# A two-layer decoder on one core: the weight pairs of the context products are multiplied with each other first, the context lies in two row halves, and the planner orders the program anew

## The reference, cut to what matters

```python
# layer 0: h = ctx_512, adj_raw = x (256 x 256 for each batch)
Q, K = h @ Wq.T, h @ Wk.T                       # 64 columns
sim = Q @ K.T / (sqrt(16) * 4)                  # summed over the heads
A = sigmoid(sim) * (sim >= 76th largest of the row)
x = layernorm(x + (1 - gamma) * x + gamma * (A + A.T) / 2)
# layer 1: k_v = ctx_512, p = x
kv  = k_v @ W_k.T + b_k
out = p @ kv
sim = out @ kv.T * 256 ** -0.5
x = layernorm(x + softmax(layernorm(sim) * ln_gamma + ln_beta))
```

## Time and profile before

| | us |
|---|---|
| runs of the kernel | 700.29, 702.64, 703.87: median 702.64 |
| profiled execution, its own time | 702.17 |
| its span, first to last instruction | 700.4 |
| PE busy | 680.6 |
| DVE, ACT, POOL busy | 531.1, 494.1, 394.8 |

### The profile page before, as it was taken

The page is one execution under the profiler, slowest core; times in us unless marked ns, Lnnn a source line. Parts: engine busy times, 40 slices in busy tenths (PEclk is TensorE's granted clock), DMA queues, the critical chain, the costliest instruction groups (busy, mean ns, idle before and its releaser), DMA issues.

```text
span 700.4 us, 14717 instructions
## 1 busy us (share of the span) xinstructions
PE 680.6 (97%) x4886; PEld 574.7 (82%) x4886; DVE 531.1 (76%) x1677; ACT 494.1 (71%) x1276; POOL 394.8 (56%) x657
## 2 busy tenths in 40 slices
PE   8899999999999999999998999999989999999995
PEld 6578998888888888888886888898977787678885
DVE  2678989888697869878889776565689777866537
ACT  3789774888659784788879786646766686857631
POOL 4659732885267741698867655544791322435625
PEclk9999999999999999999999999999999999999999
DMA  8671001240341401122012002111120000101201
GB/s 293 167 229 42 17 1 40 53 122 2 109 133 32 122 1 54 46 54 61 2 49 89 1 28 63 47 46 46 46 91 3 5 2 4 48 1 46 91 1 60
DMA packets 34418, 41.06 MB, mean 59 GB/s; under 512 B 6620, under 2 KB 27238, under 8 KB 34344
## 3 DMA queue, kind: packets, MB, share of 16 engines
q1 hardware_dynamic: 33800, 39.80, 19.4%
q10 hardware_dynamic: 544, 0.33, 0.2%
HBM read 30.02 MB, written 1.05 MB: 44 GB/s over the span
## 4 chain that ended last, share of the span: by engine, by line
PE 77%; POOL 9%; DVE 8%; issue 3%; DMA 1%; SPq 1%; ACT 0%; POOLq 0%; DVEq 0%
PE bank L1184 68%; PE bank L1198 8%; POOL stat L2341 3%; POOL qT L2341 1%; PE bank L1455 1%; POOL probs L2338 1%; DMA qT<-xT_plain 1%; DVE top_tok L2238 1%; POOL probs L2341 1%; POOL w_split_lo L2341 1%; DVE g_pair_lo L1896 1%; SPq L2622 1%; DVE y L1899 1%; POOL stat L2338 1%; DVE bn L1911 1%
## 5 line engine op out<-in xcount | busy, mean ns | idle before, releaser
L2338 POOL TENSOR_SCALAR probs<-probs,soft 128x256 f32<-128x256 f32 (+1 forms) x256 | 104.5, 429 | 48.4 <-DVE soft L2031 46.7
L1686 ACT ACTIVATE probs<-probs,soft 128x256 f32<-128x256 f32 (+1 forms) x256 | 113.0, 447 | 13.5 <-DVE soft L2023 12.9
L1184 PE MATMUL bank<-xT_hi,w_split_hi 128*128 128x512 f32 x256 | 103.7, 405 | 3.5 <-POOL w_split_lo L2341 3.2
L2341 POOL TENSOR_TENSOR w_split_lo<-w_raw,w_split_hi 128x512 fp32r<-128x512 f32 (+2 forms) x57 | 72.3, 1275 | 55.1 <-ACT w_split_hi L1592 54.9
L1184 PE MATMUL bank<-xT_lo,w_split_hi 128*128 128x512 f32 x256 | 101.0, 394 | 0.0
L1184 PE MATMUL bank<-keyT,qT 128*128 128x256 f32 (+1 forms) x512 | 93.4, 330 | 0.5 <-POOL qT L2341 0.3
L2023 DVE CUSTOM_DVE_ANT_0 probs<-bank,mask 128x256 f32<-128x256 f32 (+1 forms) x256 | 78.9, 353 | 19.8 <-PE bank L1184 19.1
L1184 PEld LDWEIGHTS bank<-keyT,qT 128*128 128x128 f32 x512 | 81.8, 190 | 12.3 <-issue 2.5
L2341 POOL TENSOR_TENSOR qT<-qT,xT_plain 64x512 f32<-64x512 f32 x44 | 57.0, 1295 | 57.6 <-DMA qT<-xT_plain 55.5
L1184 PE MATMUL bank<-xT_hi,w_split_lo 128*128 128x512 f32 x192 | 75.9, 395 | 0.0
L1592 ACT ACTIVATE qT<-bank 64x512 f32<-64x512 f32 (+1 forms) x80 | 47.4, 592 | 33.1 <-PE bank L1184 30.6
(11 more groups left out here) (240 smaller groups left out, 1822.0 us busy)
## 6 DMA issues: line engine op xcount, KB each, us to landing
qT<-xT_plain SPq DMA_DIRECT2D x88, 64.0 KB, 2.0
w_raw<-in_w_nopeT SPq DMA_DIRECT2D x8, 512.0 KB, 3.6
w_raw_heads<-in_w_o SPq DMA_DIRECT2D x8, 512.0 KB, 5.1
qT<-rope_buf SPq DMA_DIRECT2D x40, 64.0 KB, 2.0
w_raw<-in_w_gateT SPq DMA_DIRECT2D x8, 256.0 KB, 2.8
w_raw<-in_w_upT SPq DMA_DIRECT2D x8, 256.0 KB, 3.3
w_raw<-in_w_downT SPq DMA_DIRECT2D x8, 256.0 KB, 3.8
w_raw<-in_L_ffn_Wup SPq DMA_DIRECT2D x7, 256.0 KB, 2.8
```

The lines of the kernel that those rows point to most:

```text
L1184: return t.matmul(out, lhsT, rhs, start=start, stop=stop, skip_group_check=shared)
L1686: ins = s.activation(p[:, at], p[:, at], ACT.Exp, bias=st[:, 0, r:r + 1], scale=-1.0, accum_out=st[:, 1, r:r + 1])
L2338: return g_.tensor_scalar(out, in0, s1, s2, op0, op1)
L2341: return g_.tensor_tensor(out, in0, in1, op)
```

## The change

Since Q K.T = h (Wq.T Wk) h.T, and kv = [c, 1] [W, b].T, the weights can be multiplied with each other first, on PE:

- a new step `mix_x`: Wq.T Wk (64 x 64, stored twice, in partitions 0 to 63 and 64 to 127), [W, b].T [W, b] (65 columns, also twice) and its last column. Three calls and two ACT copies;
- `adj_q` replaces both `adj_qk`: only one side is multiplied, by the mixed weights. `adj_sim` takes `ctxT` itself for the other;
- `ctxT` lies as 128 partitions x 512: the first two batches in the upper row half, the last two in the lower. `adj_q` and `ctx_T` issue one product of 512 columns for each half, each into its own bank;
- `ctx_tok` and its DVE add are gone: `bi_kv` multiplies the context's own rows, loaded as `ctx_rows` with a 65th column of ones (POOL memset), and gives 65 rows. The mixed weights of layer 1 make up for it in `ctx_T`, whose result `kvT` has 65 rows;
- `xattn` has four DMAs instead of six, `ctx_rows` is one more (256 KB, in pieces of 256 bytes), and `w_down0` comes by one DMA from ACT's queue instead of two;
- the warm-up waits for the memset of `ones1` alone, reads only it, and has nine products instead of eight;
- `NEAR` and the whole table `URGENT` have new values, so that every engine's order changes throughout.

```diff
-N_WARM = 8
+N_WARM = 9
-    NEAR = {"PE": 0.0, "ACT": 0.3, "DVE": 0.3, "POOL": 0.5, "SP": 0.3, "DMA": 0.1, "WAY": 0.0}
+    NEAR = {"PE": 0.05, "ACT": 0.2, "DVE": 0.3, "POOL": 0.5, "SP": 0.3, "DMA": 0.05, "WAY": 0.0}
     URGENT = {
...
-    for i in range(2):
-        stage(("adj_qk", i), "PE 1.8, ACT 1.1", ("load", "xattn"), ("load", "ctx"), By(("down_T", 1), "PE"), ...
+    stage(("mix_x",), "PE 0.6, ACT 0.5", ("load", "xattn"), holds=[bank("mix_x", left=(("mix_x",), "ACT"))])
+    stage(("adj_q",), "PE 0.95, ACT 1.1", ("mix_x",), ("load", "ctx"), ...
-    stage(("ctx_tok",), "PE 2.5, DVE 0.6", ("load", "xattn"), ("load", "ctx"), By(("down_T", 1), "PE"), ...
-    stage(("ctx_T",), "PE 1.8, ACT 1.1", ("load", "xattn"), ("load", "ctx"), By(("down_T", 1), "PE"), ...
+    stage(("ctx_T",), "PE 0.95, ACT 1.1", ("mix_x",), ("load", "ctx"), ...
-    ctxT = sb("ctxT", [CTX, T])
-    kv_tok = sb("kv_tok", [P, NT, CTX])
-    kvT = sb("kvT", [CTX, T])
+    ctxT = sb("ctxT", [P, HALF])
+    ctx_rows = sb("ctx_rows", [P, NT, CTX1])
+    kvT = sb("kvT", [CTX1, T])
...
+    def ctx_half(h):
+        return slice(h * CTX, (h + 1) * CTX)
...
-                            mm(bank_of(("low", tile))[:, :], ones1[:, :], bias1[:, 0:2 * D])
+                            mm(bank_of(("low", tile))[:, :].rearrange("p (i s) -> p i s", s=P), ones1[:, :],
+                               ones1[:, :].unsqueeze(1).to_broadcast([P, TH, P]))
...
+                mm(out[:, 0:CTX], w_q_x[:, :], w_k_x[:, :])
+                mm(out[:, CTX:CTX + CTX1], w_kv_x[:, 0:2 * CTX], w_kv_x[:, CTX:])
+                mm(out[0:CTX1, CTX + CTX1:CTX + CTX1 + 1], w_kv_x[:, CTX:], w_kv_x[:, 2 * CTX:]).then_inc(mix_x_ready.sem, 1)
...
-                    out = wait_bank(("adj_qk", i, h))[0:CTX, :]
-                    mm(out, w_qk_x[:, i, :], ctxT[:, h * HALF:(h + 1) * HALF]).then_inc(adj_qk_ready.sem, 1)
+                    rows = ctx_half(h)
+                    out = wait_bank(("adj_q", h))
+                    mm(out[rows, :], mix_x[rows, 0:CTX], ctxT[rows, :]).then_inc(mix_x_ready.sem, 1)
...
-                    mm(out, qk_x[:, 0, tile * P:(tile + 1) * P], qk_x[:, 1, cols(b)]).then_inc(sim_ready.sem, 1)
+                    mm(out, q_x[rows, first + i * P:first + (i + 1) * P], ctxT[rows, first:first + S]).then_inc(sim_ready.sem, 1)
...
-                for tile in range(NT):
-                    ins = mm(out[:, tile, :], ctxT[:, tile * P:(tile + 1) * P], w_kv_x[:, :])
-                ins.then_inc(ctx_tok_ready.sem, 1)
...
-                    out = wait_bank(("ctx_T", h))[0:CTX, :]
-                    mm(out, w_kv_x[:, :], ctxT[:, h * HALF:(h + 1) * HALF]).then_inc(ctx_T_ready.sem, 1)
+                    rows = ctx_half(h)
+                    out = wait_bank(("ctx_T", h))[0:CTX1, :]
+                    mm(out, mix_x[rows, CTX:CTX + CTX1], ctxT[rows, :]).then_inc(ctx_T_ready.sem, 1)
...
-                    ins = mm(out, kv_tok[:, TB * b + c, :], xT[:, c, cols(b)], c == 0, c == DC - 1)
+                    ins = mm(out, ctx_rows[:, TB * b + c, :], xT[:, c, cols(b)], c == 0, c == DC - 1)
...
-                    for dst, src in ((w_down0[:, :, Q0:], a["L0_attn_q_a_w"]), (w_down0[:, :, 0:Q0], a["L0_attn_kv_a_w"])):
-                        s.dma_start(dst, src.rearrange("(c p) n -> p c n", p=P)).then_inc(loaded["low"], 16)
+                    s.dma_start(w_down0[:, :, :], a["w_low"].rearrange("(c p) n -> p c n", p=P)).then_inc(loaded["low"], 16)
...
-                own(g_.memset(plain(ones1[:, :]), 1.0))
+                g_.memset(plain(ones1[:, :]), 1.0).then_inc(unit_set.sem, 1)
...
-                g_.memset(plain(bias1[:, :]), 0.0).then_inc(unit_set.sem, 1)
+                own(g_.memset(plain(bias1[:, :]), 0.0))
...
+                own(g_.memset(ctx_rows[:, :, CTX:], 1.0))
...
-            "xattn": [(w_qk_x[:, 0, :], a["L0_xattn_WqT"]), (w_qk_x[:, 1, :], a["L0_xattn_WkT"]),
-                      (gate_col[:, 0:1], a["gamma_raw"].partition_broadcast(P)),
-                      (w_kv_x[:, :], a["L1_xattn_WkT"]), (kv_bias_col[:, :], a["L1_b_col"]),
-                      (kv_bias_row[:, :], a["L1_xattn_b_k"].partition_broadcast(P))],
+            "ctx_rows": [(ctx_rows[:, :, 0:CTX], a["ctx"].rearrange("(t p) c -> p t c", p=P))],
+            "xattn": [(w_q_x[:, :], a["w_q_x"]), (w_k_x[:, :], a["L0_xattn_Wk"]), (w_kv_x[:, :], a["w_kv_x"]),
+                      (gate_col[:, 0:1], a["gamma_raw"].partition_broadcast(P))],
```

More of the change, by code:

```diff
@@ L26 @@
 CTX = 64
+CTX1 = CTX + 1
 NH, QLR, KVLR, DR, DN, DV = 32, 192, 64, 64, 128, 128
@@ L392 @@
 LOADS_AFTER = [("xT0", "xT1"), ("xT1", "xT2")] + [("xT2", name) for name in (
-    "const", "identity", "x", "ctx", "xattn", "attn1", "router")]
+    "const", "identity", "x", "ctx", "ctx_rows", "xattn", "attn1", "router")]
 def make_plan():
@@ L469, in make_plan @@
     stage(("adj_gate",), "ACT:exp 0.3, DVE 0.8", ("load", "xattn"))
-    for i in range(2):
-        stage(("adj_qk", i), "PE 1.8, ACT 1.1", ("load", "xattn"), ("load", "ctx"), By(("down_T", 1), "PE"),
-              holds=[bank("adj_qk", i, h, left=(("adj_qk", i), "ACT")) for h in range(NHALF)], items=2)
+    stage(("mix_x",), "PE 0.6, ACT 0.5", ("load", "xattn"), holds=[bank("mix_x", left=(("mix_x",), "ACT"))])
+    stage(("adj_q",), "PE 0.95, ACT 1.1", ("mix_x",), ("load", "ctx"),
+          holds=[bank("adj_q", h, left=(("adj_q",), "ACT")) for h in range(NHALF)])
     for b in range(B):
-        stage(("adj_sim", b), "PE 1.06, ACT:exp 1.55", ("adj_qk", 0), ("adj_qk", 1),
+        stage(("adj_sim", b), "PE 1.06, ACT:exp 1.55", ("adj_q",),
               *[("adj_mask", b - 1, i) for i in range(TB) if b],
@@ L482, in make_plan @@
               holds=[bank("adj_T", b, left=(("adj_T", b), "DVE"))])
-    stage(("ctx_tok",), "PE 2.5, DVE 0.6", ("load", "xattn"), ("load", "ctx"), By(("down_T", 1), "PE"),
-          holds=[bank("ctx_tok", left=(("ctx_tok",), "DVE"))])
-    stage(("ctx_T",), "PE 1.8, ACT 1.1", ("load", "xattn"), ("load", "ctx"), By(("down_T", 1), "PE"),
-          holds=[bank("ctx_T", h, left=(("ctx_T",), "ACT")) for h in range(NHALF)], items=2)
+    stage(("ctx_T",), "PE 0.95, ACT 1.1", ("mix_x",), ("load", "ctx"),
+          holds=[bank("ctx_T", h, left=(("ctx_T",), "ACT")) for h in range(NHALF)])
     def stat(step, reader, engine="ACT"):
@@ L577, in make_plan @@
         transposed("bilinear", b, "ACT", ("bi_norm", b))
-        stage(("bi_kv", b), "PE 0.9, ACT 0.4", ("xT", "bilinear", b), ("ctx_tok",), *[By(("bi_sim", b - 2), "PE")] if b >= 2 else [],
+        stage(("bi_kv", b), "PE 0.9, ACT 0.4", ("xT", "bilinear", b), ("load", "ctx_rows"), ("zero",), *[By(("bi_sim", b - 2), "PE")] if b >= 2 else [],
               holds=[bank("bi_kv", b, left=(("bi_kv", b), "ACT"))])
@@ L943, in write_program @@
     loaded = {n: dma_semaphore(f"loaded_{n}") for n in
-              ("xT0", "xT1", "xT2", "low", "const", "identity", "x", "ctx", "xattn", "attn1", "router")}
+              ("xT0", "xT1", "xT2", "low", "const", "identity", "x", "ctx", "ctx_rows", "xattn", "attn1", "router")}
     raw_loaded = [[dma_semaphore(f"raw{i}_{part}") for part in "ab"] for i in range(2)]
@@ L1069, in bank_left @@
             "pv": lambda: ctx_lo[tuple(k)], "out": lambda: y_added[tuple(k)],
-            "adj_qk": lambda: adj_qk_copied[tuple(k)], "adj_sim": lambda: sim_copied[tuple(k)],
-            "adj_T": lambda: adj_done[tuple(k)], "ctx_tok": lambda: kv_tok_done[0],
+            "mix_x": lambda: mix_x_copied["mix"], "adj_q": lambda: mix_x_copied[k[0]], "adj_sim": lambda: sim_copied[tuple(k)],
+            "adj_T": lambda: adj_done[tuple(k)],
             "ctx_T": lambda: ctxT_copied[k[0]],
```

154 lines of the change are left out of this document (73 added, 81 removed), and 39 rows, old and new, of the table URGENT.

## The result

The changed kernel took 705.45 us in the median of 10 runs (703.15 to 706.63), the kernel before 702.76 (10 runs, 700.29 to 704.43): ratio 1.0039, with an interval of 1.0025 to 1.0053. The forecast was 697.0 us within 692 to 701.5, with chances of 0.73 for faster, 0.20 for a difference under 0.5% and 0.07 for slower. The measured difference is under 0.5%, but its interval lies above 1, and the time lies outside the range. The profiled execution of the changed kernel took 705.85 us, its span 703.7 (before: 700.4).

A forecast was written before the change was run, and what follows sets the result against it. PE, busy for 97% of the span, was taken to bound the kernel. From the profiled 702.17 us, 4.4 of PE work and 0.8 at the head were subtracted, 0 for the order: 697.0 us, range 692 to 701.5.

The forecast's parts named there:

- PE's work: On PE, 7.57 us of products removed and 3.15 added: net 4.4 us less (2.4 to 4.9).
- I put nothing down: `bi_kv` and `bi_sim` with 65 columns or rows for 64: no cost counted, 0 to 0.5 us allowed.
- The head: Earlier warm-up and one weight DMA start `down` and the queries sooner: 0.8 us gained (0 to 1.2).
- Does it reach the end?: PE's saving in attention and at the hand-over shortens the span: 4.4 us counted in full, 2 us likely loss at the edge.
- rival 3: Saving turns into PE waits at 33 and 46 us (1.1 + 1.9) and the hand-over (1): 701.4 us, chance 0.2.
- 2.4 us of new context products can fill until then: Before the queries near 33.7 us, the new context products can occupy PE until `xT_lo` is written at 32.2.
- I put 0 in the sum: The new order of every engine's steps, throughout the kernel, was counted as 0 us.
- My lean of 0.5 to the gain: For the new order, a lean of 0.5 us to the gain: more gaps to close than work to disturb.
- Rival 4: Query swaps behind weight loads on SP stall PE at three attention crossings, up to 3.2 us each: 707 us, chance 0.08.
- `ctx_rows` behind SP's queue: The 256 KB load delays what stands behind it by 0.9 to 1.8 us; nothing counted if put behind `ctx`.

The follow-up runs named there:

- e8: e3 with the products of `adj_q` and `ctx_T` issued twice; 700.21 us, ratio 0.9958 to the kernel before.
- e12: e3 with the products of `pv` 3 6 issued twice, just behind the closing adjacency transposes; 700.85 us, ratio 0.9976 to the kernel before.
- e3: The changed kernel's operations in the order and layout of the kernel before; 700.76 us, ratio 0.9973 to the kernel before.
- e1: The changed kernel with 2016 bytes left free behind `kvT`, restoring the old addresses of later tensors; 703.18 us, ratio 1.0014 to the kernel before.
- e4: The operations and layout of the kernel before in the changed kernel's order; 706.3 us, ratio 1.0049 to the kernel before.
- e6: The kernel before with 32 bytes left free ahead of `x`, so `xT` and `w_split` both move; 703.96 us, ratio 1.0020.
- e2: The kernel before with 32 bytes left free behind `kvT`, moving all later tensors; 704.99 us, ratio 1.0031.
- e7: The kernel before with 32 bytes left free ahead of `x` and 32 behind `kvT`; 703.83 us, ratio 1.0017.

## Why the prediction was wrong, step by step

- **PE's work: right where it was priced.** Forecast were 4.4 us less and a busy time of 675 to 677. With the old layout and order it is 674.9. `mix_x` cost 0.7 for 0.75, `adj_q` and `ctx_T` together 2.08 for 2.4. The up to twofold speedup that the Trainium skill gives for 64 rows (TensorEngine Tiling, Theoretical Speedup) holds here for float32: eight records in two row halves in 2.08 us, where four in one half took 1.93. The fall of 5.7 us is larger than these give, by what layer 1 saved.
- **"I put nothing down" for `bi_kv` and `bi_sim`: wrong, to the good.** For the 65th row and column 0 to 0.5 us of cost were allowed; these steps gave about 1 us. Without this piece of luck the next step would have missed by more.
- **The head: right.** First record 0.97 for 0.96, `down` 4.98 for 5.0 to 5.5, queries 0.8 us sooner, and 1.0 over all profiles.
- **"Does it reach the end?": the first failed step.** I counted the 4.4 us in full. In the old order they became the waits at 31, 45 and 356 us that rival 3 names, with 1.48 for its 1.1, 1.86 for its 1.9, and 1.8 (2.03 less the 0.27 of before) for its 1. For two of the three e8 and e12 show that work put back there is free; for the one at 31 us none was put back. I had written down what fills PE there (queries that can't start before 32.2) and set it against "2.4 us of new context products can fill until then", but in the changed kernel and in e3 these stand at 41 us, behind the queries, and only `mix_x` ahead of them. Whether `adj_q` could have stood there was not tried. Size: of 5.2 us with the head, 1.9 came, 3.3 less.
- **"I put 0 in the sum" for the order: the second failed step.** It is +2.9 us (e3 to e1), made of -1.6 in attention and +4.5 behind. My lean of 0.5 to the gain had the wrong sign; the trace of before could not have told it, but it could have told that 0 was no safer than +3, and the range ended at 701.5. Rival 4, the one slower case, had the wrong place: in attention nothing got worse.
- **The layout: not in the prediction at all.** +1.8 us (e1 to the changed kernel). The diff shows three tensors of other sizes, and I priced only their instructions.
- The three make 3.3 + 2.9 + 1.8 = 8.0 of the 8.4 us, each uncertain by 1.5 to 2. The split between the first two depends on the way taken: over e4 the order costs 3.4 us (1.0049) and the new work brings 2.5 (e4 to e1) of its 5.2.
- `ctx_rows` behind SP's queue cost nothing that a wait shows; it landed in 4.4 us.

Open are which of the new priorities puts `xT_lo` late at 379 us, what makes up the rest of the 3 us in layer 1 beside the 1.95 of idle time, why e6 is slower than its records say, and what of the low clock is the order's and what chance: a stretch lies now here, now there, from one execution to the next.

## What to carry to other kernels

A saving on the bound engine counts only if what follows it in that engine's order was already released. For each removed piece ask who waits right behind it, and for how long it had covered him; this trace told it, and the named waits came out to within 0.8 us. A change of shape by one row is a term as well, and can be a gain. A new schedule is a term with an error of its own, and can be tested by replay: an order can be taken from the one kernel, work from the other, and the best splice may beat both. When a tensor changes its size, look at where the later ones land. And before two profiles are compared at one place, see whether the clock ahead of it was the same; if not, look for a pair where it was.

## What the runs showed of the hardware

- A float32r matmul of 512 columns takes 0.2300 us from start to start when both operands stand at the same place modulo 64 bytes in SBUF (0.229 to 0.232 by tensor), and 0.233 to 0.234 when they are 32 bytes apart, whichever of the two moves (e2, e6, e7). With 256 columns the mean hardly changes (0.1167 and 0.1170), but it mixes 0.119 for operands at the same place modulo 128 bytes (`g_pair`, before), 0.118 at 32 bytes' distance (e2) and 0.115 at 64 (e7).
- Float32 products of 64 rows in the two row halves overlap almost fully: sixteen records of 512 columns in 3.80 us (e8), 0.24 each, where eight in one half took 3.64, 0.455 each. The block holds both diagonal quarters (`adj_q`) and 65 weight columns (`ctx_T`).
- A step of four float32 records of 256 columns that stands between full-array products takes 1.06 us up to the next one with 64 rows, and 0.67 with 65 (`bi_sim` at 635.80 before, at 634.44 in e3). So a lone product in half of the rows can cost more than one in slightly over half.
- The granted clock falls to its lower level of 1.2 GHz behind waits of PE, the shortest 0.88 us (e4, at 44), but not behind each: after 2.25 us at 379 it fell (375 to 400 at 0.93), after 1.48 us at 31 it didn't. The Trainium skill (TensorE: Matmul & The Clock Gate, "The HAM clock gate") calls the halved clock the idle state, and the trace agrees so far. Each stretch cost PE 1.7 us, 3.4 when it came twice in a row, though not always the kernel, as the wait at 45 us in e6 shows. It came and went between executions of one head: in e3 it stood between 24 and 28 us, in e8, with the same instructions up to there, it was absent, the clock rose sooner in `down` as well (8.85 us for its 32 records instead of 9.87), and PE came to the next queries 2.6 us sooner (28.91 for 31.47).
